# The last turn of a blocked triangular inverse taken away by exchanging the operands of one product

## The reference

```python
S = S * jnp.exp(g_t)[..., None, None]
mem = jnp.einsum('bhk,bhkv->bhv', k_t, S)
delta = (v_t - mem) * b_t[..., None]
S = S + jnp.einsum('bhk,bhv->bhkv', k_t, delta)
o_t = jnp.einsum('bhk,bhkv->bhv', q_t * scale, S)
```

## Time and profile before

| what | us |
|---|---|
| median of 3 runs (lowest, highest) | 5712.55 (5711.51, 5719.94) |
| profiled execution, span from first to last instruction | 5713.6 |
| PE busy | 5094.9, 89% |
| DVE, ACT, POOL busy | 3760.4, 2786.0, 2259.2 |
| first mixer's chunks, first turn to last L440 | 126.2 to 2953.1 |

### The profile page before, as it was taken

The page is one execution under the profiler, slowest core; times in us unless marked ns, Lnnn a source line. Parts: engine busy times, 40 slices in busy tenths (PEclk is TensorE's granted clock), DMA queues, the critical chain, the costliest instruction groups (busy, mean ns, idle before and its releaser), DMA issues. The chain is left out here.

```text
span 5713.6 us, 105779 instructions
## 1 busy us (share of the span) xinstructions
PE 5094.9 (89%) x37146; PEld 3553.8 (62%) x37146; DVE 3760.4 (66%) x8878; ACT 2786.0 (49%) x6575; POOL 2259.2 (40%) x1588
## 2 busy tenths in 40 slices
PE   5999999999899999999988998996568787998998
PEld 3776777767676776767765655653135575664665
DVE  5656656566556656556557857855679946875884
ACT  1444444444344444444437856853420024884882
POOL 2424334243324424344236725732432214752761
PEclk7999999999999999999989999997679957998998
DMA  3000000000000000000010000000000000000000
GB/s 112 5 7 7 4 7 4 7 7 4 9 4 7 4 7 6 5 7 4 7 32 1 0 24 5 0 1 6 0 8 1 1 1 29 0 23 5 0 0 15
DMA packets 170269, 53.58 MB, mean 9 GB/s; under 512 B 142224, under 2 KB 166160, under 8 KB 169232
## 3 DMA queue, kind: packets, MB, share of 16 engines
q1 hardware_dynamic: 168736, 49.54, 3.7%
q10 hardware_dynamic: 1392, 2.20, 0.1%
HBM read 41.21 MB, written 10.49 MB: 9 GB/s over the span
## 5 line engine op out<-in xcount | busy, mean ns | idle before, releaser
L342 PE MATMUL gd_ps<-gd_taps,gd_xwin 128*128 128x512 f32 x2048 | 906.5, 598 | 8.0 <-ACT gd_qT L528 8.0
L342 PEld LDWEIGHTS gd_ps<-gd_taps,gd_xwin 128*128 128x128 f32 x2048 | 382.4, 190 | 465.1 <-issue 445.6
L787 POOL TENSOR_TENSOR gd_o_rn<-gd_tmp,gd_mhalf 128x8 f32<-128x8 f32 x64 | 103.5, 1635 | 1200.5 <-DVE gd_tmp L706 1200.5
L551 ACT ACTIVATE gd_X<-gd_ps 128x512 f32<-128x512 f32 x512 | 268.2, 633 | 548.5 <-PE gd_ps L384 548.2
L1298 ACT ACTIVATE L_ffn_s<-L_ffn_s,L_ffn_nb,L_ffn_r 128x128 f32<-128x128 f32 x1024 | 419.4, 482 | 3.1
L683 DVE TENSOR_TENSOR gd_Z<-gd_ps,cst 128x256 f32<-128x256 f32 x384 | 163.0, 425 | 331.0 <-PE gd_ps L422 265.0
L1118 POOL TENSOR_TENSOR L_ffn_t<-L_ffn_t 128x512 f32<-128x512 f32 x128 | 190.4, 1488 | 397.4 <-DVE L_ffn_t L1339 397.4
L781 POOL TENSOR_TENSOR gd_gate<-gd_gate,gd_norm_w 128x2048 f32<-128x2048 f32 x32 | 145.1, 4535 | 484.2 <-ACT gd_gate L516 484.2
L384 PE MATMUL gd_ps<-cst,gd_gV 128*128 128x128 f32 x2048 | 265.4, 278 | 54.3 <-DMA gd_gV<-gd_inverses 33.4
L384 PEld LDWEIGHTS gd_ps<-cst,gd_gV 128*128 128x128 f32 x2048 | 226.3, 143 | 78.1 <-ACT gd_decay L546 75.1
L516 ACT ACTIVATE gd_v<-gd_ps 128x512 f32<-128x512 f32 x128 | 76.4, 597 | 406.2 <-PE gd_ps L342 406.2
(11 more groups left out here) (377 smaller groups left out, 13295.1 us busy)
## 6 DMA issues: line engine op xcount, KB each, us to landing
L_ffn_sb_rope<-in_rope SPq DMA_DIRECT2D x4, 2048.0 KB, 8.2
gd_tap_row<-in_L_attn_conv_v SPq DMA_DIRECT2D x2, 2048.0 KB, 7.0
gd_blocks<-gd_nA SPq DMA_DIRECT2D x256, 16.0 KB, 1.7
gd_Z<-gd_blocks SPq DMA_DIRECT2D x32, 128.0 KB, 2.0
gd_inverses<-gd_Z SPq DMA_DIRECT2D x32, 128.0 KB, 1.7
gd_gV<-gd_inverses SPq DMA_DIRECT2D x256, 16.0 KB, 2.0
L_ffn_sb_wqkv<-in_L_ffn_wqkv SPq DMA_DIRECT2D x4, 768.0 KB, 8.9
gd_tap_row<-in_L_attn_conv_q SPq DMA_DIRECT2D x1, 2048.0 KB, 15.2
```

Of the source, the lines that this page charges most:

```text
L342: ins = pe.matmul(ps[4 + i % 2][:], xwin[:, t:t + P] if i < 8 else xwin[:, PAD:PAD + P], taps[:, t, 512 * SLICE[i]:512 * (SLICE[i] + 1)] i ...
L551: act.activation(heads(X, gi).rearrange("p h x -> p (h x)"), ps[4 + gi][:], ACT.Copy).then_inc(x_s.sem, 1)
```

## The change

At the last level the second product has its operands exchanged: with `Z` as the stationary operand and the right half of `X` as the moving one it gives the turned block directly, in PSUM partitions 0 to 63 instead of 64 to 127. DVE copies it into the upper right block of `X` instead of into `Tm`. The fourth round of turns (16 transposes on PE) and ACT's four copies of it are gone, and L440, now L441, waits for DVE's copy (`Tl_s`) where it waited for ACT's (`x_s`).

```diff
-        x_mm, x_s = sig("x_mm", G * (NL + 1)), sig("X", G * (NL + 1))
+        x_mm, x_s = sig("x_mm", G * NL), sig("X", G * NL)
...
                                 if s == HALF:
-                                    ins = pe.matmul(ps[gi][HALF:P, 64 * k:64 * (k + 1)], X[:, h, HALF:P], Z[:, h], start=True, stop=True)
+                                    ins = pe.matmul(ps[gi][0:HALF, 64 * k:64 * (k + 1)], Z[:, h], X[:, h, HALF:P], start=True, stop=True)
                                 else:
                                     ins = pe.matmul(ps[gi][:, 64 * k:64 * (k + 1)], X[:, h], Z[:, h], start=True, stop=True)
                             ins.then_inc(tz_mm.sem, 1)
-                        for gi in range(G):
-                            w(Tl_s.now(n, G * l + gi))
-                            turn_T(n, gi, l + 1)
+                        if s < HALF:
+                            for gi in range(G):
+                                w(Tl_s.now(n, G * l + gi))
+                                turn_T(n, gi, l + 1)
                     for gi in range(G):
-                        w(x_s.now(n, G * NL + gi))
+                        w(Tl_s.now(n, G * (NL - 1) + gi))
                         for k in range(HG):
                             h = HG * gi + k
                             ins = pe.matmul(bank(gi)[:, k], X[:, h], R[:, h], start=True, stop=True)
...
-                    for l in range(NL + 1):
+                    for l in range(NL):
                         for gi in range(G):
                             w(x_mm.now(n, G * l + gi))
                             act.activation(heads(X, gi).rearrange("p h x -> p (h x)"), ps[4 + gi][:], ACT.Copy).then_inc(x_s.sem, 1)
...
                             if s == HALF:
-                                dve.tensor_copy(heads(Tm, gi)[HALF:P, :, 0:HALF],
-                                                ps[gi][HALF:P, 0:256].rearrange("p (h x) -> p h x", h=HG)).then_inc(Tl_s.sem, 1)
+                                dve.tensor_copy(heads(X, gi)[0:HALF, :, HALF:P],
+                                                ps[gi][0:HALF, 0:256].rearrange("p (h x) -> p h x", h=HG)).then_inc(Tl_s.sem, 1)
```

## The result

The changed kernel takes 5653.89 us in the median of 4 runs (5651.81 to 5656.78), against 5713.53 us before (5711.51 to 5719.94, 4 runs, one more than in the table above): 59.6 us less, a ratio of 0.9894 with a 95% interval of 0.9879 to 0.991. Forecast were 57.6 us less, 5655 us.

A forecast was written before the change was run, and what follows sets the result against it. PE's own issue was taken to bound the inverse's levels: 32 x 1.80 = 57.6 us for the removed round, all other terms zero, so 5712.55 - 57.6 = 5654.9 us, range 5646 to 5667 us, at 84%.

The forecast's parts named there:

- PE's issue sets the pace there, and a round is worth its start-to-start time: L422 to L440, no idle time on PE: removing the fourth round's 16 transposes saves 1.80 us per chunk, 57.6 us in all.
- Everything behind moves along: All later chains start from PE work behind the removed round, so all move by the same 1.80 us.
- the three waits: PE's first-mixer waits for normed keys (47.6 us), the small inverses' DMA (33.4) and ACT's scaled output (20.8), forecast to stay.
- L441's wait on DVE has 0.8 us of room: First DVE copy ends about 0.8 us before L441 needs it; as a rival, waiting costs 22 us, giving 5677 us, 4%.
- The 0.15 us for the signal: Signal time added to 0.54 us if L441 stood until all four DVE copies were seen: 0.7 us per chunk.
- ACT's relief gives nothing: Four ACT copies, 2.06 us, go, but PE does not wait for ACT here: no further gain.
- The exchange costs nothing: Exchanged product L429 keeps sizes and counts, 1.96 us for 32 records, so its change in cost is taken as zero.
- L431's pitch: Upper bound for the exchanged product: 0.112 us a record, 1.61 us more per chunk; as a rival 5707 us, 3%.
- The pitch itself: L429's spacing, forecast to stay at 0.061 us a record.
- The scatter from the clock: Clock falls at the two sequences' ends, one worth 7.7 us, re-dealt by the shift; part of the 5646 to 5667 range.
- the fall of the earlier trace: Before the change, last chunk: a level took 16.60 us at clock 0.51 where 8.85 us is usual.

The follow-up runs named there:

- r1: Changed kernel with PE's 16 transposes per chunk put back into PSUM banks nobody reads, without ACT's copies: 5711.23 us, ratio 1.0 to before.
- r2: Changed kernel with four ACT copies of 128x512 per chunk put back, a constant into dead tiles, without PE's round: 5645.73 us, ratio 0.9883 to before.
- r5: Changed kernel with one more DVE product of 128x256 per chunk ahead of the copies into X: 5642.39 us, ratio 0.987 to before.
- r6: Changed kernel with four more DVE products of 128x256 per chunk ahead of the copies into X: 5672.33 us, ratio 0.9922 to before.
- r4: Changed kernel with L420's fourth group and the exchanged product's first group issued in turns, head by head: 5640.92 us, ratio 0.9877 to before.
- r3: Changed kernel with the exchanged product writing PSUM partitions 64 to 127, like the product ahead; DVE copies from there: 5655.87 us, ratio 0.9899 to before.
- r7: Changed kernel with every second head's exchanged product written to PSUM partitions 64 to 127, DVE copying each group in two pieces: 5630.56 us, ratio 0.9842 to before.
- r8: Changed kernel with the first group's exchanged product in turns with L420's fourth group, other three groups split over the halves: 5624.98 us, ratio 0.9855 to before.

## Why the prediction was right

- *PE's issue sets the pace there, and a round is worth its start-to-start time.* Right: 1.80 us in r1, and the total moved by the number of chunks times what a chunk gave. That the gain was PE's alone r1 and r2 show from both sides.
- *Everything behind moves along.* Right: the three waits are unchanged in total. None of their chains begins ahead of the removed round.
- *L441's wait on DVE has 0.8 us of room.* Right: no wait in the changed kernel, and r5 and r6 place the room between 0.33 and 1.34 us, by what shows at 0.78. The 0.15 us for the signal was too much here: in r6 L441's weight load starts 0.05 us after the first copy's end (592.67, 592.72), though behind L629 it was 0.14 us (626.94, 627.08).
- *ACT's relief gives nothing.* Right (r2). It went into a wait of 3.3 us per chunk.
- *The exchange costs nothing.* This term was mis-sized. The bounds were set at zero and at L431's pitch, and so the side below zero was left out, though the trace had no 64-column product behind one of the other half, and the prediction said so. Measured: 0.18 us won per chunk by the overlap of L420 and L429 (3.70 against 3.88 us), 0.1 us lost at L441. Together 0.08 x 32 = 2.6 us, so the sum by rows is 60.2 us (32 x 1.88, the difference of the steps) where 57.6 were forecast and 59.6 measured. The pitch itself was right: L429's last 29 records take 587.59 - 585.80 = 1.79 us, 0.062 us each. (By the single records it is 0.058 us before and after, and 0.15 from the last to the product behind.) From L429's first record to L441 it is 2.01 us and not 1.96, since the first three stand among L420's.
- *The scatter from the clock.* It was needed for single runs: beside r1 to r4 the kernel before alone spread over 22 us. That the median came within 1 us of the forecast is partly luck. r2 and r5, with the same step as the changed kernel, had medians 8.2 and 11.5 us lower. And in the two profiled executions the clock fell in different places: the mixer's last step took 98.08 us before (the fall of the earlier trace rows) and 87.35 after, which with the last round is 10.7 us, yet from the last L396 to the end it is 2802.3 and 2800.0 us, only 2.3 less.

The Trainium skill's page "TensorEngine Tiling (Array Packing)", section "Key Properties", says that different tiles can run their weight loads and matmuls in parallel. The trace agrees (L429's first records among L420's last, and r3, which takes that away). It bore on the one term that was mis-sized.

What stays open: why L441 takes 0.1 us more. r1 and r3 place it at the change from the 64-column product to the full one, and the trace places it between L441's first and second record (0.21 us, where the later ones are 0.11 apart); its cause wasn't tried.

## What to carry to other kernels

Where PE's timeline shows no idle time from one piece to the next, a removed round of instructions is worth its start-to-start time, not its durations, times the passes; check then that every later wait hangs on work behind it. A product whose two operands have 64 columns each gives its result turned for the same price if the operands are exchanged, which saves the turn and its copy. And products with 64 stationary columns are worth ordering so that neighbours write different halves of PSUM's partitions: here that gave another 0.6 us of 3.7 per chunk (r7), a third of what the removed round gave. How far it goes is set by the engine that feeds and empties them: in r7 the product by R waits for DVE's copy, and in r8 the last group for its mask.

## What the runs showed of the hardware

- Two float32 products with 64 stationary columns, one writing partitions 64 to 127 and the next 0 to 63, overlap without any help from the program: three records of L429 started among the last three of L420, which the program has ahead of them. Issued in turns, they kept 0.058 us from record to record on each half at the same time (r4), the pace of a half alone.
- A full product of 128 columns straight behind a 64-column one took 0.1 us more than behind full transposes (3.67 against 3.58 us, r1 and r3).
- DVE copied PSUM partitions 64 to 127 into partitions 0 to 63 of SBUF in 0.43 us a copy (r3), as long as the copies before the change, which stayed in partitions 64 to 127.
